# Adaptive-norm attention with routed experts: the low halves of the weight splits three steps behind the high halves, splits at new steps

## The reference

```python
h = layernorm(x) * (1 + ca) + sa
x = x + ga * attention(h)           # 16 heads of 16, causal softmax
h = layernorm(x) * (1 + cb) + sb
logits = h @ router_w.T             # 8 experts, the best one per token
xr = h * sigmoid(best logit)
routed = (up * silu(gate)) @ down_proj[e]        # gate, up = xr @ gate_up_proj[e]
shared = (silu(h @ shared_gate_w) * (h @ shared_up_w)) @ shared_down_w
x = x + gb * (shared + routed)
```

## Time and profile before

| | us |
|---|---|
| median of 3 runs | 482.43 (481.32 to 484.14) |
| the profiled execution | 480.72 |
| its span, first to last instruction | 479.0 |

### The profile page before, as it was taken

How to read it: one execution, slowest core, us unless ns; L and a number is a source line. 1 busy time by engine, 2 the same in 40 slices (tenths; PEclk the granted TensorE clock), 3 DMA queues, 4 the chain that set the end, 5 groups by cost and what they waited for, 6 DMA issues and landing times.

```text
span 479.0 us, 8599 instructions
## 1 busy us (share of the span) xinstructions
PE 407.9 (85%) x3009; PEld 230.4 (48%) x3009; DVE 311.2 (65%) x635; ACT 228.5 (48%) x408; POOL 208.2 (43%) x251
## 2 busy tenths in 40 slices
PE   3886996889789989968979968999968999999991
PEld 3243453334444445424534435565645666666661
DVE  7786495567789777979887743789734444444441
ACT  2534546766475856656667626345122232323220
POOL 2488542632227943258242762110600455555332
PEclk9999998997989999988999979999989999999997
DMA  8465278585934287672354201994621344434210
GB/s 260 159 156 111 70 158 247 170 229 184 288 127 145 84 230 188 225 281 88 125 167 163 70 0 47 359 342 178 177 88 45 65 77 86 74 78 78 36 21 0
DMA packets 46193, 67.97 MB, mean 142 GB/s; under 512 B 5380, under 2 KB 33668, under 8 KB 46152
## 3 DMA queue, kind: packets, MB, share of 16 engines
q1 hardware_dynamic: 40472, 58.76, 39.7%
q0 software_dynamic: 5152, 8.14, 8.4%
q10 hardware_dynamic: 528, 0.52, 0.3%
HBM read 43.14 MB, written 25.18 MB: 143 GB/s over the span
## 4 chain that ended last, share of the span: by engine, by line
PE 46%; DVE 15%; DMA 11%; POOL 7%; issue 6%; ACT 5%; SPq 4%; ACTq 0%; DVEq 0%; POOLq 0%
PE bank L1505 34%; DVE mx L1139 4%; DMA qk_d<-W 3%; DMA w_d<-rowg 3%; DMA ng_d<-negm 3%; PE bank L1661 3%; PE bank L1886 2%; SPq L511 2%; PE bank L1645 2%; ACT rowg L950 1%; SPq L528 1%; DMA stage<-in_gup 1%; DVE rowg L1240 1%; POOL W L772 1%; DVE W L1240 1%
## 5 line engine op out<-in xcount | busy, mean ns | idle before, releaser
L900 ACT ACTIVATE W<-bank 128x512 f32<-128x512 f32 (+1 forms) x176 | 94.5, 562 | 58.5 <-PE bank L1645 57.1
L1139 DVE TENSOR_REDUCE mx<-bank 128x1 f32<-128x384 f32 (+3 forms) x176 | 105.1, 633 | 21.2 <-PE bank L1618 13.3
L1505 PE MATMUL bank<-W 128*128 128x256 f16 (+2 forms) x756 | 106.8, 295 | 8.2 <-POOL W L746 3.7
L1505 PEld LDWEIGHTS bank<-W 128*128 128x128 f16 x756 | 74.0, 100 | 42.3 <-issue 11.5
L772 POOL TENSOR_SCALAR_AFFINE_SELECT W<-W 128x512 f32<-128x512 f32 x64 | 45.5, 714 | 87.9 <-ACT W L900 87.9
L1645 PE MATMUL bank<-W 128*128 128x512 f16 (+3 forms) x256 | 65.3, 313 | 17.4 <-ACT W L900 15.0
L1505 PE MATMUL bank<-W,h2T 128*128 x276 | 67.2, 380 | 4.9 <-DVE W L1255 3.9
L843 POOL DMA_INDIRECT out<-h2T,sidx x23 | 36.3, 1578 | 69.7 <-DVE h2T L1475 69.4
L1616 PE MATMUL bank<-W 126*128 126x128 f16 (+3 forms) x208 | 54.6, 314 | 4.6 <-DVE mx L1139 4.5
L1661 PE MATMUL bank<-W 128*32 128x128 f32 (+3 forms) x512 | 50.8, 472 | 7.9 <-POOL W L772 7.9
L1645 PEld LDWEIGHTS bank<-W 128*128 128x128 f16 x256 | 22.0, 100 | 56.0 <-ACT W L900 33.2
(11 more groups left out here) (173 smaller groups left out, 548.5 us busy)
## 6 DMA issues: line engine op xcount, KB each, us to landing
w_d<-rowg SPq DMA_DIRECT2D x18, 512.0 KB, 5.7
W<-w_d SPq DMA_DIRECT2D x18, 512.0 KB, 8.0
stage<-in_gup SPq DMA_DIRECT2D x16, 512.0 KB
qk_d<-W SPq DMA_DIRECT2D x48, 128.0 KB
W<-qk_d SPq DMA_DIRECT2D x32, 192.0 KB, 4.6
stage<-in_down SPq DMA_DIRECT2D x8, 512.0 KB
x_sb<-in_x SPq DMA_DIRECT2D x4, 512.0 KB, 9.3
h_d<-gbb SPq DMA_DIRECT2D x4, 512.0 KB, 4.6
```

Of the source, the lines that this page charges most:

```text
L900: a.activation(PT[j][:, i:i + m, :], t_bank(N)[:, 0:m * w].rearrange("p (i n) -> p i n", i=m), ACT.Exp).then_inc(s_exp, 1)
L1139: v.tensor_reduce(mx_v[:, b % 2, hp0 // 4, par, i:i + m, t], s_bank(N)[:, 0:m * w].rearrange("p (i n) -> p i n", i=m), AX.X, ALU.max).then ...
L1505: i = t_.matmul(outp, l, r, start=(n == 0), stop=(n == len(prods) - 1), **kw)
```

## The change

Three edits. The steps of the splits move (loop 3 keeps its own): the first splits of loop 0 come earlier, the later ones of loop 1 later. VectorE does the low half of a split three steps after ScalarE's high half, no longer at the same step. SP's `HALVES` are adapted. And TensorE starts the gate half of routed tile 0 when hidden unit 14 is done, and waits for unit 15 only ahead of routed tile 1.

```diff
 SPLITS = {-1: {},
-          0: {16: 0, 20: 1, 25: 2, 30: 3, 35: 4, 40: 5},
-          1: {3: 6, 7: 7, 11: 8, 16: 9, 20: 10, 24: 11},
-          2: {2: 12, 7: 13, 12: 14, 16: 15, 20: 16, 23: 17, 28: 18, 33: 19},
+          0: {9: 0, 15: 1, 21: 2, 27: 3, 33: 4, 39: 5},
+          1: {2: 6, 9: 7, 15: 8, 21: 9, 27: 10, 33: 11},
+          2: {2: 12, 7: 13, 12: 14, 17: 15, 21: 16, 25: 17, 30: 18, 35: 19},
           3: {1: 20, 5: 21, 8: 22, 14: 23, 18: 24, 23: 25, 28: 26}}
-HALVES = [[[], [0, 1], [2, 3], [4]], [[5, 6, 7], [8, 9], [10, 11], []], [[12, 13], [14, 15, 16], [17], []]]
+LATER = 3
+HALVES = [[[0], [1], [2, 3], [4]], [[5, 6, 7], [8], [9, 10], [11]], [[12, 13], [14, 15, 16], [17], []]]
...
-                    if n in SPLITS[b]:
-                        split_low(SPLITS[b][n])
+                    if n - LATER in SPLITS[b]:
+                        split_low(SPLITS[b][n - LATER])
...
                     if r >= 2:
                         pe.wait_ge(s_rhid, r - 1)
-                    elif r == 0:
-                        pe.wait_ge(s_hid, NT)
+                    else:
+                        pe.wait_ge(s_hid, NT - 1 + r)
```

## The result

The changed kernel takes 488.75 us (median of 4 runs, 487.44 to 489.61) against 481.88 for the kernel before on the same chip: ratio 1.0133, 95% interval 1.009 to 1.0175. It is slower, by 6.9 us. The profiled execution took 489.61 us with a span of 487.9, which is 8.9 more than the span before, 479.0.

The account below looks back on a forecast made before the run. TensorE was taken as nearest the bound, busy 203.0 of 241.5 us in loops 0 to 3. Terms 7.8 - 1.5 + 5.5 - 2 - 2 + 0 - 0.1 = +7.7, on the median 490.1, given as 490; range 482.5 to 497.

Parts of the forecast that it names:

- Split 0, +7.8: Loop 0, step 16 to 9: ScalarE waits 11.7 us for the unmoved load; +7.0 plus 0.8 low clock, from 6 to 9.
- Splits 4, 6 and 7, -1.5: Loops 0 and 1: longer stop at split 4, split 7's wait gone; -1.5 us, from -3.3 to +2.7.
- Split 11, +5.5: Loop 1, step 24 to 33: high half waits for late write 9, a new stop; +5.5 us, from 2.5 to 8.8.
- the two terms taken off: Off the 6.6 us stop at split 11: 1.7 for idle time anyway there, 1.1 for the high half leaving step 25.
- Split 16, -2: Loop 2, step 20 to 21: about 1 us less TensorE stop, perhaps less low clock; -2 us, from 0 to -5.5.
- VectorE, -2: Low halves no longer wait for high halves, so TensorE waits less for maxima; -2 us, from 0 to -4.5.
- Loop 3, 0: Low half 22 behind the last maximum, -1.2 us; low half 25 before step 27's normalisation, delaying the mask, +1.2; together 0.
- SP's queue, 0: Loops 0 and 1: step 13's maxima, sent behind 1 MB writes and loads, just return by step 22; 0 us.
- the hand-over, -0.1: Wait for hidden unit 15: gate half starts earlier, down projection still waits for low half 15; -0.1 us, 1.7 more at most.
- The rival of late maxima: Loops 0 and 1: maxima need over 12 us to step 22, TensorE waits 2 to 3 us each; 496 us, chance 0.13.
- The rival in which only split 0 stops: Loop 1: write 9 lands by step 33, so the 5.5 us at split 11 go; 484.5 us, chance 0.20.
- The faster rival: Loops 1 and 2: VectorE runs ahead, stops at 7 and 16 vanish, split 0 costs 6 us; 475.5 us, chance 0.07.

Follow-up runs that it names:

- the kernel with both repairs: Changed kernel with first three stage loads right behind maxima(0, 0) and writes 2 and 9 ahead of the projections' writes: ratio to before 0.9855, 469.43 us.

## Why the prediction was right, and where it was not

The forecast was 490 us, +7.7, and the measurement is 488.75, +6.9. In the profiles loops 0 to 3 are 7.2 us longer, against 7.8 in the sum. The other 1.7 between the two profiles lie outside the loops, where the sum had almost nothing, and the medians are 2.0 closer than the profiles. Of the signs given, the waits at split 0 (12.2) and split 11 (5.4) came as said, and VectorE's waits for high halves are gone. Two signs failed: the wait before high half 7 did not vanish (0.9), and loop 0 is 9.5 us longer and not 6 to 8, since the longer stop at split 4 falls in it, which the sum set against splits 6 and 7 of loop 1.

**Split 0, +7.8.** Measured +7.9 by step 33 (table of shifts: 8.9 less 1.0). The working held in its numbers: the idle time of ScalarE 12.2 for 11.7, TensorE stopped before step 12 for 12.1 us. The loads at an idle place of the list then gave 10.2 us in loop 0, so the stop was worth more than its difference to the one before. The 0.8 for a longer low clock was too much: the clock was at 0.72 in the 6.7 us behind the stop, 3.7 us at 1.2 GHz, hardly more than the 3.4 of before, so 0.2 at most. But straight behind the stop, at step 18, the loss was 9.5, more than the 7.0 of the sum, and 1.6 of it came back by step 33. Most of this is where the low clock falls, by an estimate from these rows and the earlier trace rows. Here it lies ahead of step 18 and costs 1.9 there. Before it lay behind step 18, and its 1.7 are what this kernel wins back. Of the 7.9, 7.0 and 0.2 are so explained, and 0.7 are not.

```profile
69.22:81.31 12.09, 0.00 (x1) 0.01 (x1) 2.57 (x7) 1.60 (x3) 0.00 (x0) 0.59 0.84 223
81.31:88.00 6.69, 6.69 (x45) 3.34 (x45) 4.73 (x9) 4.06 (x8) 1.27 (x2) 0.72 0.48 157
```

**Splits 4, 6 and 7, -1.5.** From step 33 of loop 0 (+8.9) to step 33 of loop 1 (+7.9) it is -1.0, with the step around split 4 and the end at the same chain of DMAs as worked out. The stop at split 4, 5.56 us, lies at the upper end of what was given (2.78 and up to 2.7), and ScalarE's wait at split 7 fell to 0.9 and did not vanish. The two runs with write 2 early showed the reason given, that the chain takes up the difference.

**Split 11, +5.5.** Measured +5.2 from step 33 of loop 1 to step 0 of loop 2, and by taking the cause away 3.4 us of loop 1, or 4 to 5 us by the ratios. The write landed 5.9 us after its issue, where 6.6 to 8.2 were taken, and the stop was 4.9 and not 6.6. So the stop was 1.7 smaller and what it costs around itself 1.4 larger. Half of that is low clock, 4.9 us at 1.2 GHz at work behind the stop, which cost 2.4 where 1.7 were taken. The other 0.7 must be in the two terms taken off, and the runs don't tell which.

```profile
182.58:188.00 5.42, 5.42 (x31) 3.27 (x32) 3.84 (x6) 3.48 (x7) 0.64 (x1) 0.55 0.38 136
```

**Split 16, -2, and VectorE, -2.** The sum, -4, is what loop 2 gave, 4.4 us. The parting was wrong, so that the sum holds is in part luck. The stop at split 16 did not shrink by coming a step later, it grew, ScalarE's from 3.80 to 5.04 us and TensorE's from 2.21 to 2.85. SyncE and TensorE, and the 11 us from TensorE's stop on:

```profile
209.77 0.32 SPq L539 DMA_DIRECT2D ng_d<-negm  x1
213.71 0.55 SPq L546 DMA_DIRECT2D W<-ng_d  x2
214.73 0.50 SPq L568 DMA_DIRECT2D w_d<-rowg  x1
223.18 0.39 PE L1646 MATMUL bank<-W 128*128 128x512 f16 x1 [2.85 <-ACT W L901]
220.30:231.30 11.00, 6.76 (x57) 3.29 (x53) 10.90 (x26) 8.88 (x15) 9.32 (x12) 1.00 0.76 278
```

The step that failed is the one that took a step of delay of the split as a step less of waiting, with the landing where it was. Counted from step 0 of loop 2, ScalarE arrives 0.4 us earlier in spite of the later step (23.4 for 23.8), and the write lands 0.9 later (28.5 for 27.6). It takes 6.8 us as before, but SyncE issues it 0.9 later, behind maxima that now need 3.9 us to land where they needed 1.4. That ScalarE is early because maxima no longer hold the loop back is likely and not shown by itself; with late low halves at unmoved steps it arrives at 23.0. The gain is behind the stop. The 11 us there ran at full clock, where the earlier trace rows had 0.70, which cost 3.3 us, and the waits for maxima in loop 2 fell from 3.4 to 0.5. The kernel with only the late low halves shows a third of the gain, the spreading of the splits the rest.

**Loop 3, 0.** The last maximum gave 1.1 us, 1.2 were foreseen (+8.7 to +7.5 from step 9 to 18). The mask that I had 1.2 later came to 0.6 in the shifts (7.5 to 8.1 from step 18 to 43), and TensorE's wait for it grew by 0.2 only:

```profile
287.22 1.50 PE L1662 MATMUL bank<-W 128*32 128x384 f32 x8 [4.62 <-POOL W L773]
```

**SP's queue, 0, and the hand-over, -0.1.** Both held. The rival of late maxima was real in the kernel with the loads between the projections, where SyncE sent them 3 us later than in the one with the loads at an idle place (77.8 for 74.7), at a price of 5.0 us, about twice the 2 to 3 put on it.

The rival in which only split 0 stops had 484.5, a ratio of 1.004, and is about what the kernel with write 9 early gives (1.0041 and 1.0058), though split 4 still stops there. The faster rival had 475.5, a ratio of 0.986, and the kernel with both repairs reaches 0.9855. That is the same number by another way: the rival kept 6 us of loss at split 0 and let the stop at split 16 go, and in that kernel split 0 does not wait and split 16 waits 5.9 us.

## What to carry to other kernels

An instruction that waits for a DMA and stands in the queue of a busy engine holds up everything behind it, so before it is moved ahead, compare the time at which the engine arrives there with the time of the landing, which does not move unless its issue is moved as well. Where the stop vanishes at one place of a chain of transfers, look for it at the next: here it went from split 4 to 5 and 6, and from 6 to 7. Removing a wait of an engine that is not the bound can be worth little (23.7 us of waiting, 3 us of time). An even spread of steps is no aim where landings are not even. And a loop that is shorter in one profile is not yet a gain: 1.5 us of loop 3 came and went between two executions of one kernel.

## What was new about the hardware

The length of an idle spell of TensorE did not say what clock followed. The plainest case is one kernel, writes 2 and 9 early, in two executions. The same stop in loop 3, 4.62 and 4.63 us, was followed by 0.72 over 11 us in one and by 0.86 in the other, 6.2 and 3.1 us at 1.2 GHz, and the loops differ by 1.5 us (58.8 and 57.3):

```profile
283.63 1.51 PE L1662 MATMUL bank<-W 128*32 128x384 f32 x8 [4.62 <-POOL W L773]
283.63:294.63 11.00, 11.00 (x77) 6.67 (x77) 2.99 (x7) 2.11 (x4) 4.92 (x6) 0.72 0.01 1
281.20 1.51 PE L1662 MATMUL bank<-W 128*32 128x384 f32 x8 [4.63 <-POOL W L773]
281.20:292.20 11.00, 10.91 (x85) 6.70 (x86) 4.30 (x9) 3.60 (x7) 5.63 (x7) 0.86 0.01 1
```

At split 16 an idle spell of 2.21 us, with two more of about 1 us behind it, was followed by 0.70 over 11 us, and one of 2.85 us at the same place of the changed kernel by 1.00. And 12 us of idle time was followed by about as much low clock at work (3.7 us) as 3.85 us (3.4): most of the slow spell passed while there was nothing to do (0.59 over the 12.09 us of the stop, 9.9 us at 1.2 GHz).

A small transfer took 1.4 us or up to 8.3, by what was issued around it. The same 16 KB of maxima, in the same step of loop 0, landed 3.1 us after their issue in the changed kernel, 5.9 with the loads right behind `maxima(0, 0)`, 7.8 in the kernel before and 8.3 with the loads between the projections. Write 0 and load 3, 1 MB, are ahead of them in three of these, but issued 1.6 us ahead in the first, 1.1 in the second and 1.0 in the last, where the projections' reads had gone out just before as well; in the kernel before it is the three loads, 1.5 MB, issued in the 1.5 us before. What each of these adds was not taken apart.
